# A decoder's reciprocal standard deviations, taken from ScalarE's square root to a Newton iteration on VectorE

## The reference, cut to what matters

```python
def _layernorm(x, axis=-1, eps=1e-05):
    m = jnp.mean(x, axis=axis, keepdims=True)
    v = jnp.var(x, axis=axis, keepdims=True)
    return (x - m) / jnp.sqrt(v + eps)
```

## Time and profile before

| | us |
|---|---|
| median of 3 runs | 3250.57 (3248.42 to 3251.58) |
| the profiled execution, its own time | 3236.67 |
| its span | 3235.0 |
| TensorE busy (matmuls) | 2605.1, 81% |
| VectorE busy | 2084.5, 64% |
| ScalarE busy | 1432.6, 44% |
| GpSimd busy | 772.6, 24% |
| mean granted TensorE clock | 0.888 of full speed |

### The profile page before, as it was taken

How to read it: one execution, slowest core, us unless ns; L and a number is a source line. 1 busy time by engine, 2 the same in 40 slices (tenths; PEclk the granted TensorE clock), 3 DMA queues, 4 the chain that set the end, 5 groups by cost and what they waited for, 6 DMA issues and landing times. The chain is left out here.

```text
span 3235.0 us, 59341 instructions
## 1 busy us (share of the span) xinstructions
PE 2605.1 (81%) x19764; PEld 2168.4 (67%) x19764; DVE 2084.5 (64%) x4411; ACT 1432.6 (44%) x3352; POOL 772.6 (24%) x714
## 2 busy tenths in 40 slices
PE   5978799999743999998079999999996889976177
PEld 4866588888632999997067777777775756645032
DVE  5853689889433777775756666666665567753564
ACT  2520243343310777775444545545453466751041
POOL 0000354454115000001723323333232001110434
PEclk8987899999755999999589999999998989985595
DMA  7000000000248655664300000000002732216143
GB/s 276 0 2 0 1 1 0 0 0 0 65 190 294 266 214 215 223 223 149 104 1 1 1 0 0 0 0 0 0 0 65 229 93 88 89 32 208 68 128 117
DMA packets 165268, 270.56 MB, mean 84 GB/s; under 512 B 21088, under 2 KB 140592, under 8 KB 151856
## 3 DMA queue, kind: packets, MB, share of 16 engines
q1 hardware_dynamic: 144096, 219.84, 20.0%
q0 software_dynamic: 9216, 25.18, 2.4%
q10 hardware_dynamic: 11856, 24.26, 2.0%
HBM read 191.85 MB, written 77.37 MB: 83 GB/s over the span
## 5 line engine op out<-in xcount | busy, mean ns | idle before, releaser
L1558 ACT ACTIVATE a_prob<-a_s_ps,a_ntop 128x256 f32<-128x256 f32 x512 | 235.6, 472 | 356.2 <-DVE a_ntop L1632 356.2
L1607 POOL TENSOR_TENSOR a_prob<-a_prob,a_rden 128x1024 f32<-128x1024 f32 x128 | 242.4, 1894 | 574.4 <-DVE a_rden L1637 574.4
L2173 ACT ACTIVATE x1a_prob<-x1a_st_ps,x1a_mask_now 128x512 f32<-128x512 f32 x256 | 162.4, 687 | 89.5 <-PE x1a_st_ps L2104 87.3
L2227 DVE TENSOR_REDUCE x1a_top<-x1a_s_ps 128x4 f32<-128x1024 f32 x128 | 155.9, 1222 | 71.1 <-PE x1a_s_ps L2088 69.3
L1632 DVE TENSOR_REDUCE a_ntop<-a_s_ps 128x4 f32<-128x1024 f32 x128 | 156.3, 1221 | 68.3 <-PE a_s_ps L1483 68.3
L1145 ACT ACTIVATE x0b_sq<-x0b_f 128x1024 f32<-128x1024 f32 x64 | 67.9, 1060 | 282.0 <-DVE x0b_f L1219 281.9
L2973 POOL DMA_INDIRECT e0c_ya<-sorted_results,e_slots x64 | 68.9, 1076 | 508.6 <-POOLq L2776 489.4
L68 PE MATMUL e0x_up_ps<-e0x_xT_high,e0x_up_w_high 128*128 128x256 f32 x624 | 180.5, 289 | 1.7 <-DVE e0x_up_w_low L2904 1.7
L68 PE MATMUL e0x_up_ps<-e0x_xT_high,e0x_up_w_low 128*128 128x256 f32 x624 | 177.5, 285 | 0.0
L68 PE MATMUL e0x_up_ps<-e0x_xT_low,e0x_up_w_high 128*128 128x256 f32 x624 | 177.4, 284 | 0.0
L68 PE MATMUL e0x_y_ps<-e0x_down_w_high,e0x_hT_high 128*128 128x256 f32 x624 | 176.6, 283 | 0.0
(11 more groups left out here) (571 smaller groups left out, 8620.5 us busy)
## 6 DMA issues: line engine op xcount, KB each, us to landing
e0x_up_raw<-up_rows SPq DMA_DIRECT2D x39, 1024.0 KB, 4.8
e0x_down_raw<-down_rows SPq DMA_DIRECT2D x39, 1024.0 KB, 5.4
x_qk<-head_rows SPq DMA_DIRECT2D x384, 64.0 KB
head_rows<-x1p_rows_out SPq DMA_DIRECT2D x32, 512.0 KB, 3.8
e1w_ew<-in_L_ffn_expert_w_dram SPq DMA_DIRECT2D x8, 2048.0 KB, 18.0
sorted_tokens<-zeros SPq DMA_DIRECT2D x10, 1024.0 KB, 12.4
e0x_xg<-sorted_tokens SPq DMA_DIRECT2D x39, 256.0 KB, 2.8
sorted_results<-e0x_y SPq DMA_DIRECT2D x39, 256.0 KB, 2.2
```

Source lines behind the costliest of these rows:

```text
L1558: last = act.activation(prob[:, h % RING, n, t, :], s_ps[:, n, t * SEQ:(t + 1) * SEQ], ACT.Exp, bias=ntop[:, h % RING, n, t:t + 1], accum_ ...
L1607: last = pool.tensor_tensor(p, p, scale_of, ALU.mult)
L2173: last = act.activation(prob[:, c % 2, j, 2 * (h % 2):2 * (h % 2) + 2, :], st_ps[:, :, j * SEQ:(j + 1) * SEQ], ACT.Exp, bias=mask_now[:, p ...
L2227: dve.tensor_reduce(dst, s_ps[h % 2][:].rearrange("p n (t s) -> p n t s", t=TPB), AXIS.X, ALU.max).then_inc(s_max, 1)
```

## The change: what it does, and the diff

`norm_scales` no longer uses ScalarE. VectorE copies the variances to a tile of their own, adds eps, makes a first guess of the reciprocal root by arithmetic on the number's bits read as an integer (-0.5 times the bits plus a constant), and refines it by three Newton steps of four instructions each. With `twice` the same routine runs a second time on the variance of the normed tokens. Tile `std` goes and tile `spare` of the same size comes; semaphore `std_ready` goes. Nothing else in the program is touched.

```diff
+MAGIC = float(0x5f3759df)
+
+
+def inverse_root(engine, step, out, var, spare):
+
+
+    step.then(engine.tensor_scalar(var, var, EPS, None, ALU.add))
+    step.then(engine.tensor_scalar(out.bitcast(I32), var.bitcast(I32), -0.5, MAGIC, ALU.mult, ALU.add))
+    for n in range(3):
+        step.then(engine.tensor_tensor(spare, out, out, ALU.mult))
+        step.then(engine.tensor_tensor(spare, spare, var, ALU.mult))
+        step.then(engine.tensor_scalar(spare, spare, -0.5, 1.5, ALU.mult, ALU.add))
+        step.then(engine.tensor_tensor(out, out, spare, ALU.mult))
+
+
 def norm_scales(nc, sh, name, twice=False):
...
         var = sb("var", [P, TILES])
-        std = sb("std", [P, TILES])
         first = sb("first", [P, TILES])
-        s_dve, s_std = sem("dve_step"), sem("std_ready")
+        spare = sb("spare", [P, TILES])
+        s_dve = sem("dve_step")
         with nc.Block() as block:
 
             @block.vector
             def _(dve):
                 step = Steps(dve, s_dve)
-                step.then(dve.tensor_scalar(var[:], sh.stats[:, :, 1], EPS, None, ALU.add))
-                dve.wait_ge(s_std, 1)
-                if not twice:
-                    step.then(dve.reciprocal(sh.rstd[:], std[:]))
-                    return
-                step.then(dve.reciprocal(first[:], std[:]))
-                step.then(dve.tensor_tensor(var[:], first[:], first[:], ALU.mult))
-                step.then(dve.tensor_tensor(var[:], var[:], sh.stats[:, :, 1], ALU.mult))
-                step.then(dve.tensor_scalar(var[:], var[:], EPS, None, ALU.add))
-                dve.wait_ge(s_std, 2)
-                step.then(dve.reciprocal(std[:], std[:]))
-                step.then(dve.tensor_tensor(sh.rstd[:], first[:], std[:], ALU.mult))
-
-            @block.scalar
-            def _(act):
-                act.wait_ge(s_dve, 1)
-                act.activation(std[:], var[:], ACT.Sqrt).then_inc(s_std, 1)
+                step.then(dve.tensor_scalar(var[:], sh.stats[:, :, 1], 1.0, None, ALU.mult))
+                inverse_root(dve, step, sh.rstd[:], var[:], spare[:])
                 if twice:
-                    act.wait_ge(s_dve, 5)
-                    act.activation(std[:], var[:], ACT.Sqrt).then_inc(s_std, 1)
+                    step.then(dve.tensor_tensor(var[:], sh.rstd[:], sh.rstd[:], ALU.mult))
+                    step.then(dve.tensor_tensor(var[:], var[:], sh.stats[:, :, 1], ALU.mult))
+                    inverse_root(dve, step, first[:], var[:], spare[:])
+                    step.then(dve.tensor_tensor(sh.rstd[:], sh.rstd[:], first[:], ALU.mult))
```

## The result

| | before | after |
|---|---|---|
| median, 13 runs each | 3247.85 (3238.41 to 3251.58) | 3257.61 (3254.7 to 3262.28) |
| ratio after/before | | 1.0035, 95% interval 1.0026 to 1.0043 |
| the same two kernels once more (17 and 7 runs) | 3244.88 | 3254.57, ratio 1.0027 (1.0016 to 1.0038) |
| span of the profiled execution | 3235.0 | 3258.8 |

The account below looks back on a forecast made before the run. The six small blocks, where TensorE rests and the longest chain sets the length, were taken to bound the change: chains +12.4 us, table loads -1.28 and -0.15, so +11.0 on 3250.57 gives 3261.5 us, range 3254 to 3269.

Parts of the forecast that it names:

- The price of one step: Each waited VectorE step of the new chain costs 0.225 us (tensor_tensor) or 0.216 us (tensor_scalar).
- The six stretches: Small blocks n0 to n5, 19.6 us in all: every microsecond inside them was taken as one of the program.
- the sum: Chains in the six blocks +12.4 us, less 1.28 and 0.15 for table loads elsewhere: +11.0 us.
- rival 4: TensorE's clock shifts behind the blocks: 1.3 us either way in up to six places; widens the forecast about 3 us.
- Table loads elsewhere: ScalarE's loads outside the chains: -1.28 us at L2173, -0.15 at L518, 0 at L656.
- A dearer switch: At ScalarE's table loads: a switch costs more than its rows show, time lost beside the load; shares rival 2's chance 0.13.
- rival 2: Delay taken up behind the blocks, or table switches dearer than their rows: about +5 us, 3255.5; chance 0.13.
- the estimate of +4.1 us: Whole-program change if five departing table loads each also give back 1.38 us of drain, 6.9 us more.
- Rival 1: VectorE's chain steps overlap, at 0.09 us each: -2.9 us, 3247.7, no change to tell; chance 0.03.
- rival 3: L2173's load stays, L511's and L656's fall behind waits, guesses cost 0.7 more: up to +15.7 us, 3266.3; chance 0.12.
- The second layer's cross-attention: Stage behind n4: forecast 1.3 us shorter because the load at L2173 goes.
- Theory P: From the follow-ups, last expert layer's loop: its place in ScalarE's instruction list decides its length, not the active table.

Follow-up runs that it names:

- newton_six: Changed kernel with six Newton steps in place of three; ratio to the kernel before 1.0100 (1.0086 to 1.0114).
- newton_two: Changed kernel with two Newton steps in place of three, without the last refinement; ratio to the kernel before 1.0024 (1.0014 to 1.0033).
- switches: Changed kernel with eight small ScalarE activations, root and exponential in turn, in each small block; 3287.11 us, ratio 1.0175 (1.0157 to 1.0194).
- copies_ten: Changed kernel with ten idle 128 x 1 ScalarE copies in n5 alone; 3240.41 us in one run, last loop 93.1 us.
- copies_two: Changed kernel with two idle 128 x 1 ScalarE copies in n5 alone; 3242.64 us in one run, last loop 95.4 us.
- exp_early: tables_early plus one idle exponential ahead of the second layer's cross-attention; median 3223.69 us, ratio to the kernel before 0.9981 (0.9971 to 0.9990).
- tables_early: Kernel before, roots kept, with an idle root in the stages ahead of n0, n1, n4 and n5 to load tables early; ratio 0.9987 (0.9975 to 0.9998).

## Why the prediction was right, step by step

- **The price of one step** held: 0.216 and 0.225 us came from rows of before, and the chains of 3.29 and 7.07 us were measured as 3.30 and 7.09. The integer form has no surcharge; 0 was taken, up to 0.7 us was left open.
- **The six stretches are the program's time.** Shown, to within some 5 us in 25, by newton_six against newton_two, 24.7 us for 25.0 of chain. The chains of after and before sum to 23.57 and 11.15 us, +12.4, the sum's own number. The prediction's own sign against this step, a computing stage that became shorter by about what its block lost, half appeared: behind n1, whose chain grew by 3.5 us, the stage is 1.9 us shorter. Cover does not look like the reason, for with the 12.44 us chain of newton_six the same stage has 648.4 us. What differs is the granted clock (rival 4).
- **Table loads elsewhere.** There are 8 in place of 12, as forecast. The load at L2173 vanished, and TensorE's wait there fell by exactly 1.28 us. That these arrive at the end was assumed, not shown: the stage's length follows something else as well (below). L518 (now L520) starts without a load, 0.04 us behind the end of L467 (now L469) at 56.47 + 1.89 = 58.36; before it started at 57.11, 0.21 behind:

```profile
56.47 1.89 PE L469 MATMUL a_s_ps<-a_xT,a_qT 128*128 128x256 f32 x8
...
58.40 0.47 ACT L520 ACTIVATE a_t<-a_s_ps,a_v 128x256 f32<-128x256 f32 x1 [1.14 <-PE a_s_ps L469]
```

  The first load stands ahead of ScalarE's first copy (L507), not at L511 as I had it first, and it ran from the block's start:

```profile
47.00 1.28 ACT L509 ACT_TABLE_LOAD   x1 [46.86 <-PEq L325]
...
48.99 0.59 ACT L509 COPY a_xT<-a_wt 128x512 f32<-128x512 f32 x1 [0.70 <-PE a_wt L444]
```

  It is over at 48.28, 0.70 us before the copy begins, so it costs nothing. The load for L656 came as forecast at the block's start too (206.40), in ScalarE's idle time.
- **A dearer switch** (in rival 2) has no place in the traces: switches shows 1.50 us each, as the sum had it. The Trainium skill (ScalarE: Activation LUTs, What ACT_TABLE_LOAD costs) puts some 1380 ns of drain beside each load; the estimate of +4.1 us that the prediction made from it lies outside the first interval, 8.4 to 14.0 us. Its five loads are those that leave the chains and L2173; in number the program has four fewer.
- **Rival 1** (steps of 0.09 us) fell with the chains, and **rival 3** with the loads' places. **Rival 2** in its strong form fell with the slope of newton_six and newton_two; a microsecond or two taken up here or there it can't exclude.
- **Rival 4**, TensorE's clock, came in part. The 16 products of L668 behind n1 slowed by 1.34 us, about the price that the prediction gave a shift (1.3), and over the whole stage the clock was higher and the stage 1.9 us shorter. The granted clock of the stretches moved too (n2 from 0.61 to 0.74, n4 from 0.97 to 0.88). No run set the clock alone, so what it did to the total stays open.
- **The second layer's cross-attention**, forecast 1.3 us shorter, has 433.9 and 433.4 us where before had 438.6 and 436.8: about 4 shorter. It looked at first as if it gained 3 to 4 us from a Newton chain ahead of it (433.3 to 435.9 us in six profiles, 436.8 to 440.0 in four with roots); copies_ten and copies_two, with the same chain and no load there, have 438.2 and 437.4, so that reading fell. What its length goes with is the granted clock: the mean over the stage, by the clock records of each trace, is 0.911 to 0.918 in the five profiles with 437.0 us or more, and 0.923 to 0.929 in the eight with 436.8 or less. The 1.28 us can't be seen beside that.
- **A term that the sum lacked.** The last loop went from 95.0 and 93.8 us in the two profiles of before to 97.7 and 95.9: about +2.4 us, which the forecast did not have and the interval of the ratio (8.4 to 14.0 us) hides. The whole stage behind n5 went from 327.7 and 330.5 to 335.3 and 332.4. Theory P, the shorter list of ScalarE, would be some 2 us of this (93.8 to 95.9 us in the loop at equal clock); the rest has no cause shown.
- **How near the number came is in part luck.** Taken as means of two profiles each, the stage behind n1 and the second layer's cross-attention are together some 6 us shorter, where 1.3 were forecast, and the stage behind n5 is 4.7 us longer, where nothing was. These terms outside the chains about cancel. The chains' +12.4 us is what was understood.
- In absolute terms the forecast 3261.5 is 3.9 us above the measured median: 2.7 because the kernel before had 3247.85 over 13 runs, not 3250.57 over three, and 1.2 from the change (9.8 between the medians, 11.0 forecast). The forecast ratio is 0.0001 from the first comparison's and 0.0007 from the second's.

## What to carry to other kernels

Taking an operation off an engine is worth only what that operation really costs there. Price the new chain of small dependent steps by a waited pair from the trace (0.22 us here for an add, a product, the integer form and two operations in one alike), and compare it with what the old path costs when its one-time part is taken away. Here that part was the table load and not the root. Starting it one stage earlier, in ScalarE's idle time, is one line a place and made the kernel 0.13% faster (0.02 to 0.25), where the arithmetic that avoids the root made it 0.35% slower.

## What the runs showed of the hardware that I had not expected

- The first expert layer takes 773 to 790 us from one profile to the next, among kernels with the same code there; two profiles of the kernel before differ by 9.7 us in it. I had taken a profile's stages to be steadier than that. On chips 5 and 11 it is some 12 us shorter than on 4 and 8.
- The median of the kernel before was 3228.86 us on the chip that ran exp_early and switches, and 3244.88 to 3246.8 in the two earlier comparisons, 0.5% apart. The first expert layer may be most of that; no profile of the kernel before was taken on that chip. Ratios within a comparison are safe, absolute times across them are not.
- The last loop's length differs with ScalarE instructions in a block before it, while each of its 48 copies keeps its 372 ns: 93.1 us with ten idle copies, 95.4 with two, 95.9 with none, all at a clock of 0.96. Some us in a stage can so come with an edit that does not touch it. How is not shown.
- How TensorE's clock was granted behind a small block is no simple matter of how long it had rested. Behind n1 the first 5 us had 0.73 after 7.16 us of idle time (before), but 0.50 both after 10.69 (after) and after 6.12 (tables_early).
- A table load is issued at its block's start and does not wait for the semaphore that its activation waits for, in n0, L509 and L658; but at L2173, with two waits ahead, it came only behind TensorE's L2104.
